# Expert operands and attention buffers at other SBUF addresses in a fused attention and expert layer

## The reference

```
xn  = layernorm(x)
out = x + attn(xn) + ffn(xn)

attn: q, k, v = xn@Wq+bq, xn@Wk+bk, xn@Wv+bv      (16 heads of 16)
      scores  = (q @ k.T) * 0.95**(i-j) for i >= j, else 0
      group norm over (16 channels x 512 tokens) of (scores @ v) @ Wo + bo
ffn:  probs = softmax(xn @ gate_w)                 (8 experts)
      each expert takes, per sequence, the 128 tokens of highest probability
      y = gelu(tokens @ w1[e]) @ w2[e]             (w1: 256x1024, w2: 1024x256)
      y * probability is added to the rows of those tokens
```

## The kernel before, in words

| operand | role | before | after |
|---|---|---|---|
| w1_hi, w1_lo, even expert | stationary | 0, 0 | 0, 0 |
| w1_hi, w1_lo, odd expert | stationary | 128, 160 | 0, 0 |
| xs_hi, xs_lo | moving | 160 | 256 |
| g_hi, g_lo | stationary | 160 | 256 |
| w2_hi, w2_lo, even expert | moving | 128, 128 | 0, 0 |
| w2_hi, odd expert | moving | 160 | 0 |
| w2_lo, odd expert, first and second half | moving | 160, 64 | 0, 0 |
| xg | stationary (transposes) | 0 | 0 |
| identity in cst | moving (transposes) | 128 | 128 |
| w_hi, w_lo | stationary (L1383), moving (L1451) | 448 | 0 |
| x_hi, x_lo, a_hi, a_lo | moving (L1383), stationary (L1449 to L1453) | 96 | 0 |
| vg_hi, its two rows | moving | 448, 0 | 0, 64 |
| xn; k and o32 | stationary (transposes) | 64; 96 | 0; 0 |
| q_parity, q_decayed, k, s_sb, v_parity, k_natural | both | 96 | 0 |
| state, its two buffers | stationary (L1508) | 96, 352 | 0, 256 |

## Time and profile before

### The profile page before, as it was taken

How to read it: one execution, slowest core, us unless ns; L and a number is a source line. 1 busy time by engine, 2 the same in 40 slices (tenths; PEclk the granted TensorE clock), 3 DMA queues, 4 the chain that set the end, 5 groups by cost and what they waited for, 6 DMA issues and landing times.

```text
span 2338.6 us, 81411 instructions
## 1 busy us (share of the span) xinstructions
PE 2264.5 (97%) x34252; PEld 2095.6 (90%) x34252; DVE 1531.5 (65%) x3103; ACT 1391.5 (59%) x2553; POOL 1283.3 (55%) x2012
## 2 busy tenths in 40 slices
PE   6999999999999988999999999999999999999998
PEld 5777777777777778999999999999999999999998
DVE  3555555656666657996766767667667667676674
ACT  4555565555655546556666656666666666666664
POOL 4444444444544455655566666666566576575453
PEclk9999999999999999999999999999999999999999
DMA  3232222322223312232324324224234233232332
GB/s 120 74 95 85 75 76 83 94 84 76 76 75 94 98 61 71 49 77 50 50 44 89 46 46 91 43 49 86 47 52 82 47 54 80 48 54 43 51 50 33
DMA packets 129368, 157.72 MB, mean 67 GB/s; under 512 B 11008, under 2 KB 118656, under 8 KB 129024
## 3 DMA queue, kind: packets, MB, share of 16 engines
q0 software_dynamic: 49152, 67.14, 17.8%
q1 hardware_dynamic: 79872, 85.54, 11.6%
HBM read 85.53 MB, written 67.11 MB: 65 GB/s over the span
## 4 chain that ended last, share of the span: by engine, by line
PE 55%; DVE 0%; POOL 0%; issue 0%; ACT 0%; DVEq 0%
PE attn L1779 28%; PE scores L1698 18%; PE front L1698 7%; PE front L1688 2%; POOL out L798 0%; DVE rows L211 0%; DVE topi L207 0%; DVE top L202 0%; DVE hidden L1263 0%; DVE xs_lo L1233 0%; ACT res L949 0%; DVE rows L223 0%; PE scores L233 0%; PE scores L232 0%; DVE rows L225 0%
## 5 line engine op out<-in xcount | busy, mean ns | idle before, releaser
L1779 PE MATMUL attn<-w_hi,g_hi 128*128 128x256 f32 x2048 | 581.5, 284 | 2.5 <-DVE g_lo L1274 2.4
L1779 PE MATMUL attn<-w_lo,g_hi 128*128 128x256 f32 x2048 | 578.3, 282 | 0.0
L1779 PE MATMUL attn<-w_hi,g_lo 128*128 128x256 f32 x2048 | 578.1, 282 | 0.0
L987 ACT ACTIVATE hidden<-hidden 128x512 f32<-128x512 f32 x384 | 235.4, 629 | 263.9 <-DVE hidden L1263 263.9
L1779 PEld LDWEIGHTS attn<-w_hi,g_hi 128*128 128x128 f32 x2048 | 388.6, 190 | 3.0 <-DVE g_lo L1274 2.7
L1779 PEld LDWEIGHTS attn<-w_hi,g_lo 128*128 128x128 f32 x2048 | 388.3, 190 | 0.0
L1779 PEld LDWEIGHTS attn<-w_lo,g_hi 128*128 128x128 f32 x2048 | 388.0, 189 | 0.0
L1698 PE MATMUL scores<-xs_hi,w_hi 128*128 128x256 f32 x1280 | 362.0, 283 | 8.4 <-DVE xs_lo L1233 6.3
L1698 PE MATMUL scores<-xs_lo,w_hi 128*128 128x256 f32 x1280 | 362.8, 283 | 0.0
L1263 DVE TENSOR_TENSOR hidden<-front,hidden 128x512 f32<-128x512 f32 x256 | 176.3, 689 | 284.0 <-PE front L1698 270.7
L1698 PE MATMUL scores<-xs_hi,w_lo 128*128 128x256 f32 x1280 | 361.0, 282 | 0.0
(11 more groups left out here) (182 smaller groups left out, 5154.4 us busy)
## 6 DMA issues: line engine op xcount, KB each, us to landing
x<-in_x SPq DMA_DIRECT2D x32, 512.0 KB, 5.3
w_stage<-in_w SPq DMA_DIRECT2D x16, 1024.0 KB, 6.4
xn_rows<-xn SPq DMA_DIRECT2D x32, 512.0 KB, 3.2
res<-in_x SPq DMA_DIRECT2D x32, 512.0 KB, 3.8
out<-res SPq DMA_DIRECT2D x32, 512.0 KB, 3.4
xg<-xn_rows,step_idx POOLq DMA_INDIRECT x256
out<-y,scatter_idx POOLq DMA_INDIRECT x128, 3.9
out<-res,scatter_idx POOLq DMA_INDIRECT x128, 3.9
```

The lines of the kernel that those rows point to most:

```text
L987: act.activation(own(q, p), src, ACT.Gelu).then_inc(g_ready, 1)
L1779: last = pe.matmul(yb[k % 2][:, 0:D], g_[:, m, cols], w, start=start and m == first and i == 0, stop=end, skip_group_check=True)
```

## The change

Only addresses change: no instruction, size, semaphore or order on a queue. All hand-placed buffers of the expert stage and nearly all buffers of the attention stage get new byte addresses, the latter now by `at` and in another order. The statistics buffers of the norms and the two index buffers (`step_idx`, `scatter_idx`) move ahead of the routing tables, which shifts those, the weight stage and `res` by 768 bytes. The expert operands lie such that stationary and moving ones are 256 apart modulo 512 (table above). Its core:

```diff
-        w_hi = [None if i == 2 else sb(f"w_hi{i}", [P, DH, D], F32R) for i in range(4)]
-        w_lo = [sb(f"w_lo{i}", [P, DH, D], F32R) for i in range(4)]
-        vg_hi = sb("vg_hi", [P, DH, VG], F32R)
-        x_hi = sb("x_hi", [P, DH, S], F32R)
-        x_lo = sb("x_lo", [P, DH, S], F32R)
+        KB = 1024
+        w_hi = [None if i == 2 else at(f"w_hi{i}", [P, DH, D], F32R, o * KB)
+                for i, o in enumerate((54, 56, None, 58))]
+        w_lo = [at(f"w_lo{i}", [P, DH, D], F32R, (60 + 2 * i) * KB) for i in range(4)]
+        vg_hi = at("vg_hi", [P, DH, VG], F32R, 80 * KB)
+        x_hi = at("x_hi", [P, DH, S], F32R, 143 * KB)
+        x_lo = at("x_lo", [P, DH, S], F32R, 147 * KB)
+        a_hi = at("a_hi", [P, DH, S], F32R, 171 * KB)
+        a_lo = at("a_lo", [P, DH, S], F32R, 175 * KB)
...
-        LATE = 186880
-        w1h = [at("w1_hi0", [P, 7, QF], F32R, LATE), at("w1_hi1", [P, 7, QF], F32R, 56448)]
-        w1l = [at("w1_lo0", [P, 7, QF], F32R, LATE + K1), at("w1_lo1", [P, 7, QF], F32R, 167584)]
-        w2h = [at("w2_hi0", [P, FT, D], F32R, 78976), at("w2_hi1", [P, FT, D], F32R, 106144)]
-               for i, os in enumerate(((70784, 74880), (181920, LATE + 2 * K1 + K2 + 1088)))]
-        xs_hi = at("xs_hi", [P, 7, HALF], F32R, 87712)
-        xs_lo = at("xs_lo", [P, 7, HALF], F32R, 87712 + KX)
-        g_hi = at("g_hi", [P, FT, SL], F32R, 134816)
-        g_lo = at("g_lo", [P, FT, SL], F32R, 151200)
+        G_AT = 87 * KB + 256
+        X_AT = 143 * KB + 256
+        w1h = [at("w1_hi0", [P, 7, QF], F32R, 183 * KB + 512), at("w1_hi1", [P, 7, QF], F32R, 57 * KB)]
+        w1l = [at("w1_lo0", [P, 7, QF], F32R, 197 * KB + 512), at("w1_lo1", [P, 7, QF], F32R, 169 * KB + 512)]
+        w2h = [at("w2_hi0", [P, FT, D], F32R, 79 * KB), at("w2_hi1", [P, FT, D], F32R, 157 * KB + 512)]
+               for i, os in enumerate(((71 * KB, 75 * KB), (165 * KB + 512, 219 * KB + 512)))]
+        g_hi = at("g_hi", [P, FT, SL], F32R, G_AT)
+        g_lo = at("g_lo", [P, FT, SL], F32R, G_AT + FT * SL * 4)
+        xs_hi = at("xs_hi", [P, 7, HALF], F32R, X_AT)
+        xs_lo = at("xs_lo", [P, 7, HALF], F32R, X_AT + 7 * HALF * 4)
```

More of the change, by code:

```diff
@@ L254, in layer @@
         vec = sb("vec", [P, V_N])
+        gst_w = sb("gate_stage", [P, DH, E])
+        st = sb("ln_stats", [P, TT, 6])
+        mv = sb("ln_mv", [P, TT, 2])
+        ln_ve, ln_r, ln_y, ln_a, ln_m = (sb(f"ln_{n}", [P, TT]) for n in ("ve", "r", "y", "a", "m"))
+        ost = sb("o_stats", [P, DH, 6])
+        gm = sb("g_moments", [P, DH, 2])
+        gs = sb("g_means", [P, DH, 2])
+        gn_ve, gn_r, gn_y, gn_a, gn_m, gn_s, gn_b = (sb(f"gn_{n}", [P, DH])
+                                                     for n in ("ve", "r", "y", "a", "m", "s", "b"))
+        idx = sb("step_idx", [P, GRP], U32)
+        sidx = sb("scatter_idx", [P, GRP], U32)
         route = Routing(ctx, nc, cst)
@@ L261, in layer @@
         wst = s1[:, 0:4, :].rearrange("p a (b n) -> p (a b) n", n=D).rearrange("p (i h) n -> p i h n", h=DH)
-        gst_w = sb("gate_stage", [P, DH, E])
-        bv = sb("bv_rows", [P, D])
-        w_hi = [None if i == 2 else sb(f"w_hi{i}", [P, DH, D], F32R) for i in range(4)]
-        w_lo = [sb(f"w_lo{i}", [P, DH, D], F32R) for i in range(4)]
-        vg_hi = sb("vg_hi", [P, DH, VG], F32R)
-        xb = [sb(f"x{i}", [P, TT, D]) for i in range(2)]
-        xn = sb("xn", [P, TT, D])
-        vraw = sb("v_unbiased", [P, TT, VG])
@@ L271, in layer @@
-        st = sb("ln_stats", [P, TT, 6])
-        mv = sb("ln_mv", [P, TT, 2])
-        ln_ve, ln_r, ln_y, ln_a, ln_m = (sb(f"ln_{n}", [P, TT]) for n in ("ve", "r", "y", "a", "m"))
-        x_hi = sb("x_hi", [P, DH, S], F32R)
-        x_lo = sb("x_lo", [P, DH, S], F32R)
[L276 to L289, removed]
@@ L290, in layer @@
-        gn_ve, gn_r, gn_y, gn_a, gn_m, gn_s, gn_b = (sb(f"gn_{n}", [P, DH])
-                                                     for n in ("ve", "r", "y", "a", "m", "s", "b"))
+        KB = 1024
+        bv = at("bv_rows", [P, D], F32, 53 * KB)
+        w_hi = [None if i == 2 else at(f"w_hi{i}", [P, DH, D], F32R, o * KB)
+                for i, o in enumerate((54, 56, None, 58))]
+        w_lo = [at(f"w_lo{i}", [P, DH, D], F32R, (60 + 2 * i) * KB) for i in range(4)]
+        xb = [at(f"x{i}", [P, TT, D], F32, (68 + 4 * i) * KB) for i in range(2)]
@@ new lines, in layer @@
+        xn = at("xn", [P, TT, D], F32, 76 * KB)
+        vg_hi = at("vg_hi", [P, DH, VG], F32R, 80 * KB)
+        vraw = at("v_unbiased", [P, TT, VG], F32, 80 * KB + DH * VG * 4)
+        tm = [at(f"state{i}", [P, NSUB - 1, DH, 2 * HD], F32, 90 * KB - (2 - i) * (NSUB - 1) * DH * 2 * HD * 4)
+              for i in range(2)]
+        kn = at("k_natural", [P, TT, D], F32, 90 * KB)
+        k32 = [at(f"k{i}", [P, DH, S], F32, o * KB) for i, o in enumerate((127, 94))]
+        qd = [at(f"q_decayed{i}", [P, DH, S], F32, o * KB) for i, o in enumerate((131, 98))]
@@ new lines, in layer @@
+        qm = [at(f"q_parity{i}", [P, DH, 2, S], F32, o * KB) for i, o in enumerate((135, 102))]
+        vm = [at(f"v_parity{i}", [P, TT, VW], F32, 110 * KB + i * TT * VW * 4) for i in range(2)]
+        x_hi = at("x_hi", [P, DH, S], F32R, 143 * KB)
+        x_lo = at("x_lo", [P, DH, S], F32R, 147 * KB)
+        q32 = at("q32", [P, DH, S], F32, 151 * KB)
+        s_sb = [at(f"s_sb{i}", [P, PAIRS, 512], F32, (155 + 8 * i) * KB) for i in range(2)]
+        a_hi = at("a_hi", [P, DH, S], F32R, 171 * KB)
@@ L293, in layer @@
+        a_lo = at("a_lo", [P, DH, S], F32R, 175 * KB)
+        o32 = at("o32", [P, DH, S], F32, 179 * KB)
         tb = ctx.enter_context(nc.psum_tensor("front", [P, DH, 512], F32))
@@ L382, in layer @@
         HALF = SL // 2
-        K1 = 7 * QF * 4
-        K2 = FT * D * 4
-        KX = 7 * HALF * 4
-        LATE = 186880
-        w1h = [at("w1_hi0", [P, 7, QF], F32R, LATE), at("w1_hi1", [P, 7, QF], F32R, 56448)]
-        w1l = [at("w1_lo0", [P, 7, QF], F32R, LATE + K1), at("w1_lo1", [P, 7, QF], F32R, 167584)]
-        s2 = at("w2_stage", [P, FT, D], F32, LATE + 2 * K1)
-        w2h = [at("w2_hi0", [P, FT, D], F32R, 78976), at("w2_hi1", [P, FT, D], F32R, 106144)]
-        w2l = [[at(f"w2_lo{i}{j}", [P, FT // 2, D], F32R, o) for j, o in enumerate(os)]
-               for i, os in enumerate(((70784, 74880), (181920, LATE + 2 * K1 + K2 + 1088)))]
@@ L393, in layer @@
-        xg = [at(f"xg{k}", [P, D], F32, 53248 + 1024 * k if k < 3 else LATE + 2 * K1 + K2) for k in range(GRP)]
-        idx = at("step_idx", [P, GRP], U32, LATE + 2 * K1 + K2 + 1024)
-        sidx = at("scatter_idx", [P, GRP], U32, LATE + 2 * K1 + K2 + 1056)
-        xs_hi = at("xs_hi", [P, 7, HALF], F32R, 87712)
-        xs_lo = at("xs_lo", [P, 7, HALF], F32R, 87712 + KX)
-        xsum = at("x_sums", [P, 4, HALF], F32, 87712 + 2 * KX)
-        hid = {q: at(f"hidden{q}", [P, 2, 2, HALF], F32, o)
-               for q, o in (("22", 114336), ("21", 118432), ("11", 122528), ("12", 130720))}
@@ L401, in layer @@
-        y = [at("y", [P, GRP, D], F32, 126624), res]
-        g_hi = at("g_hi", [P, FT, SL], F32R, 134816)
-        g_lo = at("g_lo", [P, FT, SL], F32R, 151200)
+        G_AT = 87 * KB + 256
+        X_AT = 143 * KB + 256
+        w1h = [at("w1_hi0", [P, 7, QF], F32R, 183 * KB + 512), at("w1_hi1", [P, 7, QF], F32R, 57 * KB)]
+        w1l = [at("w1_lo0", [P, 7, QF], F32R, 197 * KB + 512), at("w1_lo1", [P, 7, QF], F32R, 169 * KB + 512)]
+        s2 = at("w2_stage", [P, FT, D], F32, 211 * KB + 512)
@@ new lines, in layer @@
+        w2h = [at("w2_hi0", [P, FT, D], F32R, 79 * KB), at("w2_hi1", [P, FT, D], F32R, 157 * KB + 512)]
+        w2l = [[at(f"w2_lo{i}{j}", [P, FT // 2, D], F32R, o) for j, o in enumerate(os)]
+               for i, os in enumerate(((71 * KB, 75 * KB), (165 * KB + 512, 219 * KB + 512)))]
+        xg = [at(f"xg{k}", [P, D], F32, (53 + k) * KB) for k in range(GRP)]
+        g_hi = at("g_hi", [P, FT, SL], F32R, G_AT)
+        g_lo = at("g_lo", [P, FT, SL], F32R, G_AT + FT * SL * 4)
+        hid = {q: at(f"hidden{q}", [P, 2, 2, HALF], F32, G_AT + o * KB)
+               for q, o in (("22", 32), ("21", 36), ("11", 44), ("12", 48))}
@@ L405, in layer @@
+        y = [at("y", [P, GRP, D], F32, G_AT + 40 * KB), res]
+        xsum = at("x_sums", [P, 4, HALF], F32, G_AT + 52 * KB)
+        xs_hi = at("xs_hi", [P, 7, HALF], F32R, X_AT)
+        xs_lo = at("xs_lo", [P, 7, HALF], F32R, X_AT + 7 * HALF * 4)
         xb_ = {p: sbk[:, i, :] for i, p in enumerate("AB")}
```

## The result

The changed kernel is slower. Its median is 2356.52 us (5 runs, 2352.16 to 2359.14), that of the kernel before 2343.12 us beside it (5 runs, 2338.46 to 2343.92). The ratio is 1.0054, with a 95% interval of 1.0034 to 1.0073: 13.4 us more, where 5.7 less was forecast, and over the upper end of the range. The profiled execution took 2359.14 us, its span 2357.2.

The account below looks back on a forecast made before the run. TensorE, its matmul row busy 97% of the span, was taken as the bound through the time of one matmul. From 2341.7 us, experts -8.9 and attention +3.2 gave -5.7, so 2336 us; 8-in-10 range 2314 to 2352.

Parts of the forecast that it names:

- Step 1: Expert products and downs: at distance 256 they take the floor, 280.5 ns; 8.9 us less, bounds -30 and +22 us.
- ring of 512: Expert matmuls: address differences repeat every 512 bytes, making 256 the farthest place from the bad 0.
- ring of 256: Expert matmuls: address differences repeat every 256 bytes, so 256 acts as the bad 0, near 283.3 ns.
- the cases that rest on 512: Expert matmuls, 256 good: the forecast, 0.40; load and stream never meeting, 0.20; attention products paying double, 0.08.
- seams: Expert steps: eight places where products meet downs, distance 0, staying at 283.3 ns; 1.4 us off the gain.
- rival B: Expert matmuls: places repeat every 256 bytes, all go to about 283.3 ns, +22 us, 2367 us (weaker: 2352); chance 0.16.
- Flat floor: 256-column matmuls: at every distance from 32 to 352 the recorded time is about 280.5 ns.
- a nanosecond of record is a nanosecond of span: Never-idle TensorE: recorded duration exceeds start-to-start time by a constant (281 ns against 0.12 us), so recorded savings count fully.
- The bound of the gain: Expert stage: nine matmuls without a load under them average 278.8 ns, taken as the lower bound, -30 us.
- Step 2: Attention: 1152 512-column products of L1383 go from distance 160 to 0, 2.8 ns longer each; +3.2 us.
- Step 3: Transposes, small attention matmuls, other engines and staging loads: no effect, with 2 us to either side for attention transposes.
- Rival C: Only odd experts gain, 4.6 us, attention takes 3.2 back, 2340 us; or places have no part, 2343; chance 0.16.

Follow-up runs that it names:

- e2_all_up_96: Changed kernel with every expert operand, stationary and moving, 96 bytes further up, differences kept; 2356.40 us (kernel before 2345.01).
- e6_g288_x320: Changed kernel with expert operand distances modulo 512 of 320 for products and 224 for downs; 2332.64 us (kernel before 2341.62).
- e5_both_192: Changed kernel with products and downs both at distance 192 modulo 512, weights at 320; median 2313.85 us, ratio 0.9886 to the kernel before.
- e4_g64_x192: Changed kernel with expert operand distances modulo 512 of 192 for products and 448 for downs; 2317.82 us (kernel before 2345.01).
- e12_zero: Changed kernel with products and downs both at distance 0 modulo 512; 2357.39 us (kernel before 2341.59).
- e10_g192_x448: Changed kernel with expert operand distances modulo 512 of 448 for products and 320 for downs; 2320.49 us (kernel before 2341.59).

## Why the prediction was wrong, step by step

**What bounds the kernel, and that the matmul's own time decides: right.** No engine, wait or transfer took part. The longest wait stands where it stood: `L1525` has 13.4 us in the earlier trace rows and 13.9 after.

```profile
PE attn L1525 <- issue: 13.9, 23, 2.1
```

**Which two operands meet: borne out as far as it goes.** The idea that the moving address counts against the stationary one was right (`e2_all_up_96`). That it is the next matmul's block can't be seen in the new kernels, where all blocks of one kind have the same place, but the odd experts of before show it: xs and w1_lo are at 160, w1_hi at 128. Behind `xs_lo,w_hi`, whose next block is the one at distance 0, the spacing is 120.8 ns; behind `xs_hi,w_lo`, whose own block is at distance 0 and the next at 32, it is 117.4 (recorded 284 and 280). Where `xs_hi,w_lo` ends a row and a block of g at 160 comes next, it is 121.3.

**Step 1, the price of 256: this is the step that failed.** It said: "Nearest rows: 160 on one side, 352 on the other, 281 and 281 ns; I take the floor, 280.5". They are neighbours of 256 on a ring of 512 only. On a ring of 256 the same two rows are 160 and 96, and 256 is the 0 for which the text had rows of 283 and 284. The measured value is 283.0 for products (spacing 120.0), next to the upper bound of 283.3 given there; the sum had a gain of 0.5 ns (even experts) and 1.3 ns (odd) a matmul, where a step of 22.15 us (even) and 22.29 us (odd) became one of 22.46, a loss of 1.7 and 0.9 ns. Both rings fitted all rows, as the text said, and yet the ring of 256 got 0.16 and the cases that rest on 512 most of what was left. Nothing in the trace favoured 512; it was the modulus in which the addresses had been written down. With two models equal on every row and opposite on the one new point, each should have had about half. (The seams between runs of products and downs are nine in a step, not eight; that is 0.2 us, and on the ring of 256 they are the same place as the rest.)

**The size of rival B: too large.** It gave +22 us; the experts lost 13.8 (laid over each other) to 15.4 us (by the steps). The recorded means of before had been taken as 281.4 for all. By spacing the mean matmul of before stands (22.46 - 22.22) us / 180 = 1.3 ns under the worst place, not 1.9, since the downs of before were already near it (119.2 and 119.8 of 120.7).

**"Flat floor" and "a nanosecond of record is a nanosecond of span".** The floor from 32 to 352 was read from three rows of two kinds of matmul (products and L1451), to 1 ns. Spacings over the table above range over 5.3 ns in products and 3.3 in downs. Record less spacing isn't quite constant (163.0 ns for products after, 161.8 in `e6_g288_x320`), and 1.2 ns is as much as the effect that was to be priced. Starts repeat far better: a step of the changed kernel takes 22.460 us for even and for odd experts.

**The bound of the gain, 278.8 from lone matmuls: wrong.** Products at 192 record 277 to 278 among their neighbours, load under each. A timeline of products after, then in `e5_both_192` (start, duration):

```profile
1274.80 0.28 PE L1698 MATMUL scores<-xs_lo,w_hi 128*128 128x256 f32 x1
1274.92 0.28 PE L1698 MATMUL scores<-xs_hi,w_lo 128*128 128x256 f32 x1
...
1276.00 0.28 PE L1698 MATMUL front<-xs_hi,w_lo 128*128 128x256 f32 x1
```
```profile
1260.78 0.28 PE L1698 MATMUL scores<-xs_hi,w_lo 128*128 128x256 f32 x1
1260.90 0.28 PE L1698 MATMUL scores<-xs_hi,w_hi 128*128 128x256 f32 x1
...
1261.92 0.28 PE L1698 MATMUL scores<-xs_hi,w_hi 128*128 128x256 f32 x1
```

Ten spacings take 1.20 us in the first. In the second nine matmuls stand between the two ends of 1.14 us, also ten spacings. The recorded duration of a lone matmul isn't the limit of a row of them.

**Step 2, attention: sign wrong, size harmless.** 397 became 389 to 391 and not 400, 240 ns of spacing became 234. The loads of these products are as long as those of the experts (188 ns recorded in both), and still the places act the other way round. Pricing one length by the other had no ground.

**Step 3, the rest at nothing: right** for the transposes (272 and 273), L1453 (287 against 289) and the other engines.

**The rule of two independent read ports.** Here the rows are plain: 179.68 us against 174.40 for the same 1506 instructions, by addresses alone. "TensorE: Matmul & The Clock Gate", Part 2, of the Trainium skill has it that loading the next weights takes nothing from the running matmul. By that rule all windows would be equal; the trace disagrees by 3%. Rival C, whose second half rested on it, is out: the odd experts became slower by 1.35 us and the even ones by 2.49.

**Open.** The mechanism isn't settled. No experiment says why there are two spacings and what picks one, why at 192 all rows of products take the lower in `e4_g64_x192` and `e5_both_192` and all rows of downs the upper (114.7 and 118.5 in the mean), or why 512 columns prefer 0. The attention layout of before with the new expert places wasn't tried.

## What to carry to other kernels

When a matmul stream fills TensorE, the distance of its moving operand from the next stationary block is worth 3% of the expert windows here and costs two constants to try. It repeats every 256 bytes, and for 256 columns distance 0 was the worst of eight places. Since rows of one kernel can settle at two spacings, try a placement whole; the best times of two kinds taken from two kernels don't add up. Before a period is used to interpolate, ask which shorter periods fit the same rows, and give the point on which they disagree as much chance on the bad side as on the good one. Price small effects by the spacing of starts, not by recorded durations.

## What the runs showed of the hardware

- Spacing of 256-column float32r matmuls with a 128x128 load under each, at a granted clock of 1.00: 120.0 ns at distance 0 modulo 256 (`e12_zero` and the changed kernel agree to 0.1 ns), less at every other distance tried in the mean.
- A shift of all expert operands by 96 bytes changes the window by 0.05 us (179.68 and 179.73).
- Products at 448 (192 modulo 256) settle at 113.3 or 117.8 ns, both in one kernel (`e10_g192_x448`: 125 and 110 rows), with the same difference of addresses.
- 512-column products have the opposite preference: spacing 233.4 to 234.7 ns at distance 0, 240.2 at 160 (recorded 389 to 391 and 394 to 397).
- Several matmuls pass before a row of them settles: at 192 in `e5_both_192` the first three spacings of a row are mostly 121, 122 and 116 ns, the fourth is 114 and the following 113.3.
